# Four programs on one core: the first group's loads put behind seven tiles, V's bias added through the output weights, the first shared product made in the experts' program

## What is computed

```python
    x = L0_attn_x
    xn = _layernorm(x, axis=-1)
    x = x + _L0_attn_ref(xn, L0_attn_W_qkv, L0_attn_b_qkv, L0_attn_W_out, L0_attn_b_out) + _L0_ffn_ref(xn, L0_ffn_w_gate, L0_ffn_w1_e, L0_ffn_w3_e, L0_ffn_w2_e, L0_ffn_w1_s, L0_ffn_w3_s, L0_ffn_w2_s)
```

```python
        qkv = (x @ W_qkv + b_qkv).reshape(B, T, 3, H, Dh).transpose(2, 0, 3, 1, 4)
...
        attn = jax.nn.softmax(jnp.einsum('bhqd,bhkd->bhqk', q, k) * scale, axis=-1)
        out = jnp.einsum('bhqk,bhkd->bhqd', attn, v)
        out = out.transpose(0, 2, 1, 3).reshape(B, T, C)
        return out @ W_out + b_out
...
        weights, idx = _gate(x, w_gate)
...
        routed = jnp.einsum('tef,ehf,te->th', g * u, w2_e, combine)
        shared = _swiglu(x, w1_s, w3_s, w2_s)
        return (routed + shared).reshape(shape)
```

## Time and profile before

| | us |
|---|---|
| median of three runs (1231.74 to 1236.12) | 1234.71 |
| the profiled execution | 1240.19 |
| its span in the trace | 1238.2 |
| first program, until about | 176.4 |
| second program, until about | 862 |
| third program, until about | 1120 |

### The profile page before, as it was taken

The page is one execution under the profiler, slowest core; times in us unless marked ns, Lnnn a source line. Parts: engine busy times, 40 slices in busy tenths (PEclk is TensorE's granted clock), DMA queues, the critical chain, the costliest instruction groups (busy, mean ns, idle before and its releaser), DMA issues. The chain is left out here.

```text
span 1238.2 us, 27841 instructions
## 1 busy us (share of the span) xinstructions
PE 1168.3 (94%) x8338; PEld 585.0 (47%) x8339; DVE 960.1 (78%) x1450; ACT 752.9 (61%) x1568; POOL 580.5 (47%) x861
## 2 busy tenths in 40 slices
PE   4996969999999999999999999998999999998998
PEld 2553533333333333333333333333788887774665
DVE  6464658699999999999999999980555555555888
ACT  3653522688888888888888888887333333330000
POOL 6995966444556563232313232331566666660000
PEclk9998975799999999999999999999999999998999
DMA  7465653526354433434233332402677666644775
GB/s 218 133 199 190 214 142 131 194 61 189 98 144 127 141 115 96 116 91 98 78 105 102 100 88 80 110 29 68 198 225 229 210 197 214 198 154 157 234 225 174
DMA packets 127000, 181.74 MB, mean 147 GB/s; under 512 B 41153, under 2 KB 88641, under 8 KB 124994
## 3 DMA queue, kind: packets, MB, share of 16 engines
q1 hardware_dynamic: 111554, 138.55, 38.6%
q0 software_dynamic: 15360, 42.04, 9.7%
HBM read 99.71 MB, written 80.81 MB: 146 GB/s over the span
## 5 line engine op out<-in xcount | busy, mean ns | idle before, releaser
L1048 DVE TENSOR_REDUCE mx<-pm 128x1 f32<-128x1024 f32 x512 | 621.1, 1222 | 27.5 <-PE pm L1098 26.9
L1022 ACT ACTIVATE pr<-pst 128x512 f32<-128x512 f32 x1024 | 556.6, 596 | 84.4 <-PE pst L1109 32.3
L1098 PE MATMUL pm<-kt,qt 48*128 48x512 f32 x1024 | 389.0, 463 | 14.1 <-PEq L141 7.2
L1109 PE MATMUL pst<-qt,kt 50*128 50x512 f32 x1024 | 380.2, 451 | 0.0
L1121 PE MATMUL po<-pr,vt 128*17 128x256 f32 x4096 | 325.0, 390 | 9.7 <-ACT osb L1032 9.3
L1098 PEld LDWEIGHTS pm<-kt,qt 48*128 48x128 f32 x1024 | 158.1, 193 | 239.9 <-DVE mx L1048 175.7
L1268 POOL DMA_INDIRECT s_y<-ys_c,slot_c x144 | 139.8, 971 | 86.3 <-issue 49.5
L1121 PEld LDWEIGHTS po<-pr,vt 128*17 128x17 f32 x4096 | 69.0, 95 | 200.0 <-issue 112.5
L1109 PEld LDWEIGHTS pst<-qt,kt 50*128 50x128 f32 x1024 | 153.9, 187 | 12.3 <-ACT pr L1022 10.9
L950 POOL DMA_INDIRECT s_xg<-p_rows,p_slot x128 | 125.4, 980 | 56.0 <-issue 30.2
L1345 PE MATMUL c_pG<-w13s,xt_c 128*128 x576 | 150.2, 384 | 0.1
(11 more groups left out here) (187 smaller groups left out, 1182.0 us busy)
## 6 DMA issues: line engine op xcount, KB each, us to landing
xg<-s_xg SPq DMA_DIRECT2D x144, 128.5 KB
yg<-s_y SPq DMA_DIRECT2D x32, 512.0 KB, 4.0
s_q<-stg SPq DMA_DIRECT2D x32, 256.0 KB
s_k<-stg SPq DMA_DIRECT2D x32, 256.0 KB
kt<-s_k SPq DMA_DIRECT2D x32, 256.0 KB
qt<-s_q SPq DMA_DIRECT2D x64, 128.0 KB
s_o<-osb SPq DMA_DIRECT2D x32, 256.0 KB, 7.0
w13s<-w SPq DMA_DIRECT2D x1, 4608.0 KB, 14.4
```

Source lines behind the costliest of these rows:

```text
L1022: nc.scalar.activation(pr[:, (k % 2) * 4 + ORDER[i], :], pst[bank(gg, k, i)][:, :], ACT.Exp, scale=SCALE).then_inc(exp_ok, 1)
L1048: nc.vector.tensor_reduce(mx[:, half, col:col + 1], pm[slot][:, :, :].rearrange("p a n -> p (a n)"), AX.X, ALU.max).then_inc(mx_free, 1)
L1098: mm = pe.matmul(pm[slot][:, kk, :], qt[buf][rows, half, pair, qi * P:(qi + 1) * P], kt[buf][rows, pair, kk * 512:(kk + 1) * 512], start=T ...
L1109: pe.matmul(pst[bank(buf, k, i)][:, :], kt[buf][rows, pair, kc * P:(kc + 1) * P], qt[buf][rows, half, pair, :], start=True, stop=True)\
```

## The change

Three edits, in one diff.

1. `first_loads` issues the same 13 transfers at seven places: two of the keys' in rounds 16 and 18, two of the queries' in rounds 20, 22, 24 and 26, the values' one in round 28. `load_keys` and `load_queries` take the parity as an argument.
2. The bias rows are cut to Q's and K's 512 columns, and L460's product goes; pV starts with its weights. In the third program SP loads b_v into two columns, VectorE spreads it over 128 columns (`bvs`), and TensorE multiplies it with the output weights after its last block. The fourth program's VectorE adds the result to bo first.
3. Four accumulators (`pd`) and the semaphores of gate and up are shared between the third and the fourth program; TensorE makes unit 0's pair (`shared_up`) at the end of the third.

```diff
@@ stage_a, SP
-                if k == 2 * TPB:
+                n = k - 2 * TPB
+                if n == 0:
                     for i in range(2):
                         sp.wait_ge(st_out[i], STORES * 16)
                     for i in range(TPB):
                         sp.wait_ge(v_out[i], 16)
-                    load_keys(sp, s_k, first["kt"][0], 0, first["qk_in"])
-                    load_queries(sp, s_q, first["qt"], 0, 0, first["qk_in"])
-                    load_queries(sp, s_q, first["qt"], 1, 0, first["late_in"])
+                if n in (0, 2):
+                    load_keys(sp, s_k, first["kt"][0], 0, first["qk_in"], (n // 2,))
+                if n in (4, 6):
+                    load_queries(sp, s_q, first["qt"], 0, 0, first["qk_in"], (n // 2 - 2,))
+                if n in (8, 10):
+                    load_queries(sp, s_q, first["qt"], 1, 0, first["late_in"], (n // 2 - 4,))
+                if n == 12:
                     load_values(sp, s_v, first["vt"], 0, 0, first["v_in"])
@@ stage_a, PE
-                pe.matmul(pV[t % 2][:, 0:C + E], ones3[:], bias3[:, 2 * C:W], start=True, stop=False)
                 for c in range(CC):
                     mm = pe.matmul(pV[t % 2][:, 0:C + E], xt[:, t, c, :], wsb[:, c, 2 * C:W],
-                                   start=False, stop=(c == CC - 1))
+                                   start=(c == 0), stop=(c == CC - 1))
@@ stage_c, SP, then DVE (in normalise), then the end of PE
+            for c in range(CC):
+                sp.dma_start(bv[:, c:c + 1], b_qkv[2 * C + c * P:2 * C + (c + 1) * P].rearrange("(p a) -> p a", a=1))\
+                    .then_inc(bv_in, 16)
+                if k == 2:
+                    dve.wait_ge(bv_in, 16 * CC)
+                    nc.vector.tensor_copy(bvs[:], bv[:].unsqueeze(2).to_broadcast([P, CC, P])).then_inc(bvs_ok, 1)
+            pe.wait_ge(keep["xT_in"], 16 * 2 * B)
+            pe.wait_ge(xt_ok, NX)
+            shared_up(pe, keep, 0)
+            pe.wait_ge(bvs_ok, 1)
+            pe.wait_ge(hb_ok, NX)
+            for c in range(CC):
+                pe.matmul(keep["pd"][2][:, 0:C], bvs[:, c, :], keep["w_out"][:, c, :], start=(c == 0), stop=(c == CC - 1))
@@ stage_d, DVE, then PE
+            own.link(v.tensor_tensor(bo[:], pG[2][:, 0:C], bo[:], ALU.add))
             straight(NT, PER, [(0, gated), (DOWN, output), (SUM, combine)])
-                u, b = k // 2, k // TPB
-                if k % TPB == 0:
-                    pe.wait_ge(keep["xT_in"], 16 * 2 * B)
+                u = k // 2
+                if u == 0:
+                    return
+                if u == 1:
+                    pe.wait_ge(dve_own, 1)
                 need(pe, h_ok, u - 1)
```

More of the change, by code:

```diff
@@ L151, in stage_a @@
         wsb = sb("wsb", [P, CC, W])
[L152 to L155, removed]
+        brow = sb("brow", [1, 2 * C])
+        brest = sb("brest", [1, 2 * C])
+        bparts = [sb(f"bpart{n}", [1, 2 * C], BF16) for n in range(3)]
+        bias3 = sb("bias3", [3, 2 * C], BF16)
         ones3 = sb("ones3", [3, P], BF16)
@@ L732, with load_rows_of @@
 K_RUNS = [(0, 2, 1), (0, 1, 1)]
-def load_rows_of(eng, src, dst, runs, gi, done):
-    for par in range(2):
+def load_rows_of(eng, src, dst, runs, gi, done, pars=(0, 1)):
+    for par in pars:
         row = par * LANE
@@ L1180, in load_token_tile, with stage_c @@
         .then_inc(keep["x_in"][k % BUF_X], 16)
-def stage_c(nc, x, s_xt, s_o, s_rec, s_xg, s_y, keep):
+def stage_c(nc, x, b_qkv, s_xt, s_o, s_rec, s_xg, s_y, keep):
     PER, HALF = 8, 4
@@ L1201, in stage_c @@
         ident = keep["ident"]
-        pT, pG, pH, pY = ([ctx.enter_context(nc.psum_tensor(f"c_{n}{i}", [P, 512], F32)) for i in range(2)]
-                          for n in ("pT", "pG", "pH", "pY"))
+        pT, pG = keep["pd"][0:2], keep["pd"][2:4]
+        pH, pY = ([ctx.enter_context(nc.psum_tensor(f"c_{n}{i}", [P, 512], F32)) for i in range(2)]
+                  for n in ("pH", "pY"))
+        bv, bvs = sb("bv", [P, CC]), sb("bvs", [P, CC, P])
+        bv_in, bvs_ok = sem("bv_in"), sem("bvs_ok")
         slot_ok = sem("c_slot_ok")
@@ L1361, in _, with shared_up @@
             steps(pe, NX // PER, PER, NX, [(0, look_up), (0, turn), (DOWN, down), (HT, turn_h), (UP, up)])
+            pe.wait_ge(keep["xT_in"], 16 * 2 * B)
[5 more added lines that the diff above has]
+                pe.matmul(keep["pd"][2][:, 0:C], bvs[:, c, :], keep["w_out"][:, c, :], start=(c == 0), stop=(c == CC - 1))
+def shared_up(pe, keep, u):
+    g, b, w13 = u // 2, u // 4, keep["w13"]
+    for gu, done in enumerate((keep["gate_ok"], keep["up_ok"])):
+        for c in range(CC):
+            mm = pe.matmul(keep["pd"][u % 2 * 2 + gu][:, :], w13[:, c, E + u % 2, gu * F:(gu + 1) * F],
+                           keep["xT"][b][:, c, g % 2 * QH:(g % 2 + 1) * QH], start=(c == 0), stop=(c == CC - 1))
+        mm.then_inc(done, 1)
 def stage_d(nc, x, s_y, out, keep):
@@ L1368, in stage_d @@
         sem = lambda n: ctx.enter_context(nc.semaphore(n))
[L1369 to L1370 removed]
+        w2, wo, bo = keep["w2"], keep["w_out"], keep["b_out"]
+        ot, xr, x_in = keep["ot"], keep["xr"], keep["x_in"]
         yg = sb("yg", [P, BUF_Y, TOPK, C])
@@ L1375, in stage_d @@
         ys = keep["spare"][:, 1, :, :]
-        pG, pA = ([ctx.enter_context(nc.psum_tensor(f"d_{n}{i}", [P, 512], F32)) for i in range(4)]
-                  for n in ("pG", "pA"))
+        pG = keep["pd"]
+        pA = [ctx.enter_context(nc.psum_tensor(f"d_pA{i}", [P, 512], F32)) for i in range(4)]
+        gate_ok, up_ok = keep["gate_ok"], keep["up_ok"]
         yg_in = [sem(f"yg_in{i}") for i in range(BUF_Y)]
         y_out = [sem(f"yd_out{i}") for i in range(4)]
-        gate_ok, up_ok, sg_ok, h_ok, pa_ok, acc_ok, ys_ok = (
-            sem("d_" + n) for n in ("gate_ok", "up_ok", "sg_ok", "h_ok", "pa_ok", "acc_ok", "ys_ok"))
+        sg_ok, h_ok, pa_ok, acc_ok, ys_ok = (sem("d_" + n) for n in ("sg_ok", "h_ok", "pa_ok", "acc_ok", "ys_ok"))
         dve_own = sem("dve_own_d")
@@ L1459, in up @@
                     return
-                u, b = k // 2, k // TPB
-                if k % TPB == 0:
-                    pe.wait_ge(keep["xT_in"], 16 * 2 * B)
-                need(pe, h_ok, u - 1)
-                for gu, done in enumerate((gate_ok, up_ok)):
-                    for c in range(CC):
-                        mm = pe.matmul(pG[u % 2 * 2 + gu][:, :], w13[:, c, E + u % 2, gu * F:(gu + 1) * F],
-                                       xT[b][:, c, g % 2 * QH:(g % 2 + 1) * QH], start=(c == 0), stop=(c == CC - 1))
-                    mm.then_inc(done, 1)
+                u = k // 2
[3 more added lines that the diff above has]
+                    pe.wait_ge(dve_own, 1)
+                need(pe, h_ok, u - 1)
+                shared_up(pe, keep, u)
             def down(k, t, g):
@@ L1529, in program @@
         free = [t[:].bitcast(F32) for t in first["kt"]] + [first["qt"][:].rearrange("p a b t -> p a (b t)").bitcast(F32)]
+        keep.update(pd=[ctx.enter_context(nc.psum_tensor(f"pd{i}", [P, 512], F32)) for i in range(4)],
+                    gate_ok=ctx.enter_context(nc.semaphore("d_gate_ok")), up_ok=ctx.enter_context(nc.semaphore("d_up_ok")))
         keep.update(xT=free + [sb("xT3", [P, CC, T])[:]])
-        stage_c(nc, x, s_xt, s_o, s_rec, s_xg, s_y, keep)
+        stage_c(nc, x, b_qkv, s_xt, s_o, s_rec, s_xg, s_y, keep)
         stage_d(nc, x, s_y, out, keep)
```

17 lines of the change are left out of this document (6 added, 11 removed).

## The result

The changed kernel takes 1222.31 us (median of 5 runs, 1219.42 to 1225.57) against 1234.71 (now 5 runs, 1231.74 to 1236.12): a ratio of 0.991, 95% interval 0.9891 to 0.9929. Forecast were 1229.0 and a range of 1221 to 1234.5: the time lies in the range, but the step down is 12.4 us where 5.7 were forecast. Between the two profiled executions the difference is 1240.19 - 1225.57 = 14.6 us, more than between the medians; part of that is chance, as will be seen.

The account below looks back on a forecast made before the run. Stores were taken to pace the first program's second half, and TensorE the last program. Terms -1.3 + 0.3 - 4.7 = -5.7 us gave 1229.0 at the median (1234.5 for an execution like the profiled one); range 1221 to 1234.5.

Parts of the forecast that it names:

- rival 1: First program: DMA engines have room, so spread loads are hidden; -15.4 us there, 1215 in all, half hidden 1222; chance 0.15.
- the first program's term: Projections: 14.1 us of spread loads, less 14.0 at one place, less 1.4 for V's bias product, giving -1.3 us.
- The loads in series: First program: loads queue with stores on shared DMA engines; 10.1 us repeated query loads plus 4.8 for the rest, together 14.9.
- the slack: First program's store blocks: room for loads up to 1.6 us over three blocks, of which half, 0.8, was taken.
- the two narrow engines: First program: four repeated query loads use two of sixteen DMA engines at 52 GB/s, among the eight that staging stores use.
- 2, slower: First program: SP's issuing adds to engine time, +6.0 us, 1237.9 in all; sign: store block over 23 us behind another; chance 0.08.
- 3, only the seam: First program within 0 to +2 us, seam at its poor end: -1 to -3, 1231.5 to 1234 in all; chance 0.27.
- V's bias: First program: removing one 0.21 us product per tile counts only for seven tiles before stores bind, worth 1.4 us.
- The two expected signs that failed: First program: ScalarE's store waits sum to 12 to 18 us in pieces of at most 7; its end moves under 3 us.
- The sign about small stores: First program: SP issues no small store that takes over 4 us.
- The seam: Experts to shared program: first shared pair made early; -5.4 us at full clock, -4.0 if the clock falls; -4.7 taken.
- Start of the experts: Third program: VectorE waits for two added small loads and copies 128x256; +0.3 us, ends 0 and +1.

Follow-up runs that it names:

- second profile: The changed kernel run again unchanged, on the chip of the one-part-undone runs: 1220.35 us, ratio 0.9892 to the kernel before; its profiled execution took 1229.13.
- the first two groups: Two sets of four follow-up kernels, each set on its own chip beside the kernel before, whose medians there were 1233.24 and 1233.79 us.

## Why the prediction was right, and where not

**In the range, in part by luck.** 1222.31 lies between 1221 and 1234.5, but the forecast itself was 1229.0 and its half chance stood on 1226 to 1231. The range reached below 1226 only for a half-hidden case of rival 1, and loads that hide behind stores are not what happened. The mechanism of the forecast was right in its three parts; the first program's term was too small by 2 to 5 us, and the number is in the range because the range had room there for another reason.

**The loads in series: right, with the bias in.** The prediction read 14.0 us off SP's queue for the loads at one place and made 14.1 of them spread, 14.9 less 0.8 of slack. At one place they cost 100.9 - 86.3 = 14.6 us. Spread, with the bias still in, 13.7 to 14.0, so the gain of spreading is 0.6 to 0.9 where -0.1 was forecast, and the slack, 0.8, was sized well. With the bias out the spreading gave 0.7 to 3.5 in one trace or another (101.0 less the four block times), which I can't explain: the first block starts within 0.6 us in all four, and the gain falls in the last two intervals (21.5 and 23.7 in one trace, 20.4 and 21.2 in another). That the two narrow engines are at fault is shown by the wide loads. Their price was a little too high: by 10.1 us at 52 GB/s against 1.9 at the prediction's 279 GB/s, 8.2 were to be had, and 6.5 were. All loads wide cost 94.4 - 86.3 = 8.1 us where the same prices give 6.7, so 4.8 us at 279 GB/s for the rest was too low; the two errors cancelled in the 14.9.

**The rivals.** 1, hidden loads, fell: even taken out of the first program they aren't hidden, and the 12 to 14 us gained there went into two waits of 15.4. 2, slower, fell too, though its sign was there: a block of stores came 23.7 us behind the one before (145.64), over the 23 named. The sign was badly set, since three intervals before it were short; it is the sum over the blocks that decides, 100.4 against 100.9. 3, only the seam, fell with the first program's end at 172.88.

**V's bias: the term that was mis-sized.** The prediction read 0.21 us off one row of one product and multiplied by seven tiles, 1.4. A tile became twice that shorter, 0.42 (4.22 to 3.80). The product's neighbours shrink too: V's products from 1.18 to 1.08, and 0.1 between the query products and what follows. Over six or seven tiles that is the 2.4 to 2.9 us by which the first block came earlier (48.21 to 45.28, or up to 45.8 in the other runs), and it reaches the end: 177.6 to 175.2 with the loads at one place. The prediction capped the gain by GpSimd's 4.03 us a tile; in the first seven tiles nothing of that was seen.

**First program in all:** forecast -1.3, traces -3.5 to -6.1 (first maxima 174.2, 174.0 and 171.9 against 177.6 and 178.1). The term was mis-sized by V's bias, and by the gain of 0.7 to 3.5 that spreading has once the bias is out. The two expected signs that failed belong to it: waits of 12 to 18 us in pieces of at most 7 (23.7, pieces of 8.1 and 9.1), and an end that moves by under 3 us (3.5). With the bias in, the waits did sum to 16.5 and 17.0, in pieces of up to 8.5 and 9.2. The sign about small stores held: none takes over 2 us to issue.

**The seam: right, at the full-clock end.** Forecast -4.7, between -5.4 at full clock and -4.0 if the early pair fell to half; it ran at full clock, and the traces give 15.4 to 16.2 in the five traces without it against 10.9 in every one with it and the bias product, -4.5 to -5.3. The prediction never asked what the bias product does for the clock: without it the seam is 12.1 in both kernels tried. V's bias thus paid 1.2 us at a place where it was booked as a cost.

**Start of the experts: +0.3, measured nothing.** From the last maximum to the experts' first product are 32.6 us before and after, VectorE doesn't stand for the two bias loads, and with the same clock at the start (3.4 us at half) the last scatter comes 285.4 us behind the last maximum in the kernel before and in the changed one.

**What no step had.** 0.5 us of the time around the span; and two draws of the clock, in the attention, which moves one execution by 4.4 us, and at the start of the experts, 1.1 us here. They made the profiled difference of 14.6. Carrying differences of one profiled execution to the median was safe for the forecast only because nothing of either was in it.

**What stays open.** The terms that traces show, 3.5 to 6.1, 4.5 to 5.3 and 0.5, make 8.5 to 11.9 us; the medians differ by 12.4 and 12.9. And undoing one part at a time costs 5.7, 8.1 and 7.4 us at the median, 21 in all. Of the excess of 8.3, 1.2 us at the seam are a joint effect, which two parts share and which is lost with either; in the first program it is up to 1.7 (with the changed kernel's first maximum at 171.9; none with it at 174.2). V's bias alone, without the other two parts, was not run. The rest was not settled: it is of the size by which the attention and the experts differ from one execution to the next (645.8 to 652.3 us and 284.2 to 287.0), and one trace per kernel can't average that out.

## What to carry to other kernels

Transfers that can't be hidden are made little cheaper by issuing them at several places; look at how many engines they run on. Here four loads that repeated 16 rows by a broadcast cost 6.5 us more than eight plain ones. Price a product that is removed by the distance between repeats of the whole pattern, before and after, not by its own row. Work that fills a gap of TensorE can be worth more than its own time, if it keeps the clock up for what follows: the seam took 10.9 us with the bias product and 12.1 without. And before two profiles are subtracted, compare their granted clock stretch by stretch.

## What the runs showed of the hardware that was not expected

TensorE's clock at the start of the attention is drawn: in all fourteen traces it is at half behind the first maximum, and the stretch ended 36.5 to 54.2 us after that maximum's start. In the three in which it ended earliest (36.5, 39.0 and 39.1 us) TensorE was soon waiting, 2.88, 1.82 and 1.63 us for a maximum, and the granted clock fell to half again at that wait, for 6.8, 17.0 and 17.1 us. The kernel before, first profile, and the changed one, second profile (timeline of TensorE):

```profile
227.07 0.79 PE L1098 MATMUL pm<-kt,qt 48*128 48x512 f32 x1 [1.63 <-DVE mx L1048]
```

```profile
221.32 0.79 PE L1099 MATMUL pm<-kt,qt 48*128 48x512 f32 x1 [1.82 <-DVE mx L1049]
```

In the other eleven no wait of over 1 us stands between 210 and 235 us and the clock holds once it has risen. At half clock TensorE is slow enough for VectorE to keep up; back at full clock too soon, it overtakes VectorE, stands, and is slowed again. That reading fits all fourteen traces, but no run forced it.

The experts' start is drawn too. In the ten traces of the first two groups and the first comparison TensorE was at half clock there for 0, 3.4 or 6.9 us, and the time from the last maximum to the last scatter follows: 284.2 us (one trace), 285.4 to 286.0 (five), 286.6 to 287.0 (four). The kernel before and the changed one each appear with 3.4 and with 6.9.
